# VectorE's order in a transformer layer with a ternary feed-forward product: maxima between the butterflies, output statistics behind the second heads

## What is computed

```
x = x + layernorm(attention(layernorm(x)))        # x: 8 x 1024 x 512, 16 heads of 32
x = x + layernorm(ffn(layernorm(x)))

attention: Q, K, V = x @ W.T + b;  scores = Q K / sqrt(32), causal, minus (t - t') as decay
           softmax over the keys, times V, heads joined, @ Wo.T + bo
ffn:       xh = x @ H                             # H: 512 x 512 Hadamard / sqrt(512)
           scale = max(|xh| of the row) / 7;  xq = clip(round(xh / scale), -8, 7) * scale
           wq = ternary(weight) * mean(|weight| of the row);  y = xq @ wq.T
```

## Time and profile before

| | us |
|---|---|
| median of 3 runs (lowest, highest) | 1216.96 (1216.04, 1217.57) |
| the profiled execution | 1213.31 |
| its span, first to last instruction | 1211.4 |
| PE busy | 1100.2 (91%) |
| DVE busy | 1009.3 (83%) |
| ACT busy | 702.7 (58%) |
| POOL busy | 599.1 (49%) |
| mean granted TensorE clock | 0.977 |

### The profile page before, as it was taken

The page is one execution under the profiler, slowest core; times in us unless marked ns, Lnnn a source line. Parts: engine busy times, 40 slices in busy tenths (PEclk is TensorE's granted clock), DMA queues, the critical chain, the costliest instruction groups (busy, mean ns, idle before and its releaser), DMA issues.

```text
span 1211.4 us, 44874 instructions
## 1 busy us (share of the span) xinstructions
PE 1100.2 (91%) x18625; PEld 726.4 (60%) x18656; DVE 1009.3 (83%) x2558; ACT 702.7 (58%) x1494; POOL 599.1 (49%) x719
## 2 busy tenths in 40 slices
PE   5899999999999999999999999999999999999641
PEld 3566556666666666666566666666666666666320
DVE  5749998888988888899888888988888899887772
ACT  5454566666566566655666665566566655665431
POOL 2333545555454556555545555454556555445422
PEclk9999999999999999999999999999999999999875
DMA  9746665666666576566675656656575566654230
GB/s 271 165 110 138 124 130 136 159 138 136 134 125 137 142 146 153 125 136 138 122 145 137 159 134 137 136 125 132 142 149 145 131 137 138 124 129 102 72 70 36
DMA packets 204687, 161.81 MB, mean 134 GB/s; under 512 B 150432, under 2 KB 150688, under 8 KB 204384
## 3 DMA queue, kind: packets, MB, share of 16 engines
q1 hardware_dynamic: 199600, 141.34, 55.2%
q0 software_dynamic: 4880, 17.57, 4.1%
HBM read 40.87 MB, written 16.78 MB: 48 GB/s over the span
## 4 chain that ended last, share of the span: by engine, by line
PE 56%; DVE 32%; issue 7%; ACT 2%; SPq 1%; DMA 1%; POOL 1%; POOLq 0%; DVEq 0%; ACTq 0%
PE f_job L1281 42%; DVE f_bst L980 6%; PE f_st L1382 3%; DVE f_z L1058 3%; PE f_o L1399 2%; PE f_o L1404 2%; DVE f_o L970 2%; DVE f_inverse L972 2%; PE f_job L1426 2%; DVE f_rmax L948 2%; DVE f_x L1004 2%; DVE f_folded_x L1021 2%; DVE f_y L1012 2%; DVE f_y L1011 2%; DVE f_small L1006 1%
## 5 line engine op out<-in xcount | busy, mean ns | idle before, releaser
L469 POOL TENSOR_SCALAR_AFFINE_SELECT f_PT<-f_PT 64x512 f32<-64x512 f32 (+1 forms) x256 | 202.0, 810 | 68.6 <-ACT f_PT L635 42.8
L484 POOL TENSOR_TENSOR f_square<-f_stage 128x512 bf16<-128x512 f16 x128 | 130.8, 1044 | 130.7 <-ACT f_stage L613 117.5
L1281 PE MATMUL f_job<-f_xTh,f_wqh 128*128 128x256 f16 x512 | 140.8, 275 | 15.6 <-DVE f_wkl L809 14.4
L613 ACT ACTIVATE f_stage<-f_job,f_bias 128x256 f16<-128x256 f32 x256 | 106.0, 465 | 83.7 <-PE f_job L1281 76.9
L475 POOL TENSOR_TENSOR f_OTl<-f_o,f_OTh 128x256 f16<-128x256 f32 x128 | 86.3, 674 | 114.4 <-ACT f_OTh L653 113.6
L1281 PE MATMUL f_job<-f_xTl,f_wqh 128*128 128x256 f16 x512 | 140.2, 274 | 0.0
L1281 PE MATMUL f_job<-f_xTh,f_wql 128*128 128x256 f16 x512 | 140.2, 274 | 0.0
L1281 PE MATMUL f_job<-f_xTh,f_wkh 128*128 128x256 f16 x512 | 139.9, 273 | 0.0
L1281 PE MATMUL f_job<-f_xTh,f_wkl 128*128 128x256 f16 x512 | 139.8, 273 | 0.0
L1281 PE MATMUL f_job<-f_xTl,f_wkh 128*128 128x256 f16 x512 | 139.7, 273 | 0.0
L934 DVE SCALAR_TENSOR_TENSOR f_stage<-f_job,f_bias,f_stage 128x256 f16<-128x256 f32 x256 | 110.7, 474 | 29.5 <-ACT f_stage L613 27.5
(11 more groups left out here) (181 smaller groups left out, 3026.5 us busy)
## 6 DMA issues: line engine op xcount, KB each, us to landing
f_stacks<-f_stage SPq DMA_DIRECT2D x380, 128.0 KB
f_xin<-x SPq DMA_DIRECT2D x32, 512.0 KB, 4.6
f_x<-x SPq DMA_DIRECT2D x32, 512.0 KB, 4.0
out<-f_z POOLq DMA_DIRECT2D x32, 512.0 KB, 3.3
f_Vmix<-f_V SPq DMA_DIRECT2D x32, 256.0 KB, 3.2
f_Vmix<-f_V SPq DMA_DIRECT2D x64, 128.0 KB, 3.4
f_stacks<-rows_const SPq DMA_DIRECT2D x3, 512.0 KB, 7.8
f_stacks<-wqT SPq DMA_DIRECT2D x2, 512.0 KB, 6.0
```

The lines of the kernel that those rows point to most:

```text
L469: nc.gpsimd.affine_select(out=d, in_=d, compare_op=ALU.is_ge, fill=0.0, base=odd * SUB, pattern=[[0, 4], [0, TP], [1, SUB]], channel_multi ...
L484: nc.gpsimd.tensor_tensor(square[:, 2 * m + pair, :], h, h, ALU.mult).then_inc(squared, 1)
L613: nc.scalar.activation(stage[:, 2 * m, g, :], bank("qk", g)[:, m * W2:(m + 1) * W2], ACT.Identity, bias=bias[:, m, g:g + 1]).then_inc(qk_h ...
L1281: mm = pe.matmul(dst, lhs[a](c), rhs[b](c), start=(n == 0), stop=(n == 3 * KC - 1))
```

## The change

Only the order of VectorE's calls in the main loop changes. In a step, the second `scale_out` and the first `maxima` come between the butterflies of tile 0 and those of tile 1, and the second `maxima` behind the butterflies of tile 1; `z_stats` goes behind `normalise(s, 1)`; `keep_norms` follows it, then `x2_low(k, 1)`, and `z_columns` behind that.

```
                 if has(k):
                     fold(k, 0)
                     fold_again(k, 0)
+                if has(k - 1):
+                    scale_out(k - 1, 1)
+                maxima(n, 0)
+                if has(k):
                     fold(k, 1)
                     fold_again(k, 1)
-                if has(k - 1):
-                    scale_out(k - 1, 1)
-                    z_stats(k - 1)
+                maxima(n, 1)
                 if has(k):
                     x2_low(k, 0)
                 normalise(s, 1)
-                maxima(n, 0)
-                maxima(n, 1)
+                if has(k - 1):
+                    z_stats(k - 1)
                 keep_norms(n)
+                if has(k):
+                    x2_low(k, 1)
                 if has(k - 1):
                     z_columns(k - 1)
-                if has(k):
-                    x2_low(k, 1)
                 maxima(n, 2)
                 maxima(n, 3)
                 split_max(n)
```

## The result

The change makes the kernel slower: 1262.72 us median (1261.33 to 1266.61, 4 runs) against 1216.56 (1216.04 to 1217.57, 4 runs) of the kernel before on the same chip, ratio 1.0382 with a 95% interval of 1.0367 to 1.0398. The forecast was 1253 with a range up to 1263. The median lies at its upper end, and the ratio times the 1216.96 that the forecast started from is 1263.4, just past it. So the direction was right, the loss was 46 us where 36 was said, and the range was too short at its upper end.

The account below looks back on a forecast made before the run. The bound was a loop of TensorE from `qk` to `out_product(k, 1)`, then VectorE to `keep_norms`. Late maxima 9.3 plus late columns 26.5 gave +35.8 us, added to the 1216.96 median: 1253 us, range 1226 to 1263.

Parts of the forecast that it names:

- The gate: `qk(n+1, 0)` waits until VectorE's `keep_norms` has read bank job0; TensorE's other 1.37 us of waits gather there, gain 0.
- The first maxima's wait: First `maxima`, moved forward, wait for `scores(n, 0)`: 0.18 us, or 0.82 where s is a multiple of 4; 9.3 us.
- Columns and port: `z_columns` runs behind `x2_low(k, 1)`, 0.61 us later, and POOL's masks hold L1072 and L1074: 1.52 us late.
- One-hold: Rival: POOL's mask gets in only once at the column instructions; +24 us, 1241 us, chance 0.18.
- no-port: Rival: POOL's masks do not hold the column instructions, only 0.61 us late; +12 us, 1229 us, chance 0.21.
- durations stay: For the whole change: no instruction is added or taken away, each keeps its length, only places change.
- The chain to TensorE: Late columns delay ACT's `norm_z`, `invert(s, 2)`, `front_norm` and exponentials, so `keys(s, 1)`'s second half waits 1.04 or 0.82 us.
- The slack of 0.18: VectorE's second low part already waited 0.18 us for ACT, so `front_norm` is 1.34 us late instead of 1.52.
- the upper bound's 1.22: TensorE's wait before `keys(s, 1)`'s second half with both holds and no slack: 1.22 or 1.00 us, 31.4 us.
- The sign that was named for it: Idle time before L1382, in `keys(s, 1)`, released by ACT's exponentials; its absence would refute the delay reaching TensorE.
- the columns' term: Share of the summed loss from late columns reaching TensorE at `keys(s, 1)`: 20 x 1.04 + 7 x 0.82 = 26.5 us.
- the last rival: Late queues hold TensorE too, or its clock falls in the longer idle piece: above 1263 us, chance 0.04.

Follow-up runs that it names:

- the forward product alone: Kernel before with only the second ternary product (`scale_out(k-1, 1)`) moved between the butterflies of the two tiles: 1220.13 us, ratio 1.0022.
- the filled kernel: Changed kernel with six constant-weight products ahead of `scores(n, 3)` from n = 4 on, filling TensorE's idle time before `qk(n+1, 0)`: 1253.36 us, ratio 1.0299.

## Why the prediction was right in direction and short in size

1. *The gate* held. TensorE's 1.37 us were not saved but gathered there, as one piece of 1.95 in after. The maxima's lateness of 0.2 is in it too; the remaining 0.4 I did not trace. And the forward product alone gave nothing.
2. *The first maxima's wait* was slightly undersized: 0.18 and 0.82 were said, 0.22 and 0.93 came, which makes 10.9 us for 9.3.
3. *Columns and port* happened as forecast, both holds, 0.6 us each. The rule cited from the Trainium skill (SBUF — State Buffer, "Who interferes with whom") agrees with the rows of the kernel with the masks moved too: L1063 and L1065 took 0.42 and 0.61 as soon as a mask ran beside them. One-hold and no-port rivals fall. But "durations stay" was wrong for one more instruction, L914. It reads one operand and not two, so the rule as quoted did not point at it, and in before it already took 0.50 in most steps where 0.17 is its own time.
4. *The chain to TensorE* was right in its links and too small in its size. The slack of 0.18 ahead of `front_norm` was there: VectorE's second low part starts 9.52 behind `keep_norms` in after and 8.18 in before, 1.34 late, as was said. Behind it L914 took 0.69 for 0.50, and so `front_norm` came 1.52 late. The second half of `keys(s, 1)` is 1.23 late where 1.04 was said (that the first half is 1.04 late is a coincidence), and `out_product(k, 1)` 1.29, beyond the upper bound's 1.22. The sign that was named for it, idle time before L1382 (L1384 in after), shows only in the weight loads (5.0 us in 25 waits for L635 in after's list). For most of it is not idle time before that half: 0.74 of it TensorE had already lost before `out_product(k, 0)`, to VectorE's low part, which the same delay had pushed. With the clock kept up, the steps of s = 0, 1, 2 and 3 modulo 4 are 2.28, 1.10, 1.50 and 1.44 longer than before in the filled kernel. Less the maxima's 0.22 (0.93), that leaves 30.5 us for the columns where the sum had 26.5.
5. *The steps that failed* are therefore two. The larger is the columns' term: a VectorE delay of 1.34 was handed on as 1.34, and L914's longer hold beside `heads_low` made it 1.52, which with the low part's wait cost some 4 us in all. The other is the sum's silence on the clock. It was left to the last rival, at 0.04, priced only as "above 1263". The trace of before gave no step below 1.00, and I took that to hold for idle time of any shape; it had two pieces of 0.82 and 0.55. Gathered in one piece of 1.54 to 2.32, 1.95 in the step shown, the same idle time brings TensorE to the 1.2 GHz level in nine of 27 steps, and with it work that is on the path: 4.9 us. Neither alone would have carried the time past the range.

The timeline of TensorE behind the gate in after shows products first at the spacing of before, then at twice that:

```profile
401.86 0.28 PE L1283 MATMUL f_job<-f_xTh,f_wqh 128*128 128x256 f16 x1 [1.95 <-DVE f_nmax L940]
...
402.86 0.42 PE L1283 MATMUL f_job<-f_xTh,f_wqh 128*128 128x256 f16 x1
403.07 0.42 PE L1283 MATMUL f_job<-f_xTh,f_wql 128*128 128x256 f16 x1
```

and the stretches over the same time show the clock, the first figure behind POOL's:

```profile
401.90:403.90 2.00, 2.00 (x14) 1.61 (x15) 1.97 (x4) 0.29 (x1) 2.00 (x4) 0.73 0.81 204
403.90:405.90 2.00, 2.00 (x12) 1.37 (x9) 1.23 (x6) 1.97 (x5) 0.28 (x1) 0.50 0.86 61
405.90:408.00 2.10, 2.10 (x50) 1.31 (x49) 2.03 (x5) 0.99 (x4) 1.77 (x2) 0.92 0.61 124
```

The traces' account for steps 4 to 30 closes: 944.6 us before, 986.0 with the clock kept up, 990.9 in after. That is 41.4 where 35.8 were said, from the two undersized terms (1.6 and 4.0), plus 4.9 for the clock. Outside these steps the trace of after is another 7.1 us longer, where the prediction had 0. That was not looked into; it may lie in the choice of execution, since the profiled one of after lies 3.9 above its median and that of before 3.7 below. Without the clock's part the kernel runs at 1253.36, the forecast's own number, but by chance: 5.6 us were missing from the terms, while the medians of before lie 3.7 above its profiled execution and that of the filled kernel 3.3 below its own.

In after a step at 0.95 is 0.1 to 0.8 us longer than its kind at 1.00. In the kernels where TensorE has no wait behind the gate it is 1.3 to 1.7. Part of the difference shows in the rows: in all nine such steps of after L914 takes only 0.28 to 0.50, since POOL's and VectorE's instructions meet at another moment. That TensorE's waits behind the gate take up the rest is likely and not shown.

## What to carry to other kernels

Here the idle time that two small waits shared cost its length at most; the same time gathered in one piece in front of a gate also cost the clock behind it, in a third of the steps. So look at the largest single idle piece that a move of waits makes, and leave room for it in the range. Before moving an early operation forward, look for the next reader in the ring that opens later: here only the kernels that moved the maxima and `keep_norms` together, with the statistics ahead of both, gained anything. When a small piece is put behind a large one, follow it through every queue that waits in order for it. Columns that came 1.5 us late cost some 20 us because ACT's queue had another group's work behind their consumer, and one swap on ACT took 17.7 of it back in one kernel and 21.7 in the other. Late statistics held POOL's masks, and through them TensorE, as soon as TensorE no longer waited elsewhere. And when two engines' instructions can hold each other, don't take their durations over from the trace of before: a shift by 0.02 us in who starts first was worth 0.37 us of a step.

## What was not expected of the hardware

- TensorE's granted clock fell to 0.50 of full speed, its 1.2 GHz level, about 1 us after it had started again behind 1.95 us of idle time, in some steps and not in others with the same idle time (the next step stood idle 1.96 and stayed at 1.00). Of the 27 steps from s = 4 on, none showed it in before, with single pieces up to 0.82; two with pieces before `scores(n, 2)`, behind 2.03 and 1.53, while 17 others with 1.27 to 1.53 stayed at 1.00; one behind a piece of 2.00 before `weigh(s, 3)`, while all with 1.21 to 1.65 there stayed; nine with 1.54 to 2.32 at the gate, and all but two with 2.35 to 3.03 there. In steps 2 and 3 single falls show in several kernels, with only the edit on ACT too, and were not looked into. What decides between equal steps, and whether the place in the step matters beside the length, stays open.
- An instruction of VectorE on two columns takes as long as POOL's large instruction that started before it, 0.55 to 0.70 us instead of 0.15 to 0.17. That holds for masks (L469) and for `heads_low` (L475), and for L914, which reads a single operand. With starts 0.02 us apart the order of the two decides: 0.69 or 0.17. In the one kernel that moved POOL's masks another small instruction was held instead, and it was the slowest of all, at 1284.76.
